# Next x late, routing early, block sums moved on VectorE, and the base bias added by GpSimd

## The reference, cut to what matters

```python
w = weight[adapter_ids]                        # one of 8 matrices, 1024 x 1024, for each batch element
y = einsum('bsi,boi->bso', x, w)               # x: 8 elements x 256 tokens x 1024
base_out = y @ base_W.T + base_b
logits = y @ router_W.T + router_b             # 15 experts, mapped onto 8
probs = softmax(logits)                        # the 8 largest kept, summed by mapped expert: gates
h = y @ A.T                                    # 8 experts x rank 16 = 128 columns
lora = ((h * gate) @ B) * 2.0
out = x + base_out + lora
```

## Time and profile before

| | us |
|---|---|
| median of 3 runs | 430.16 (429.05 to 432.26) |
| profiled execution: time | 432.55 |
| profiled execution: span from first to last instruction | 430.7 |
| busy in the span: PE, PEld, DVE, ACT, POOL | 404.3, 373.5, 295.6, 154.9, 0.8 |
| mean granted TensorE clock | 0.988 of full speed |

### The profile page before, as it was taken

One profiled execution on the slowest core, in us unless ns is written; L12 is line 12 of the kernel. 1 busy time (PEld: TensorE's weight loads), 2 busy tenths in 40 slices (PEclk: granted clock), 3 DMA queues, 4 the chain that ended last, 5 costly groups with the idle time before them and its releaser, 6 DMA issues.

```text
span 430.7 us, 6373 instructions
## 1 busy us (share of the span) xinstructions
PE 404.3 (94%) x2272; PEld 373.5 (87%) x2272; DVE 295.6 (69%) x577; ACT 154.9 (36%) x238; POOL 0.8 (0%) x8
## 2 busy tenths in 40 slices
PE   6989969998599998999999999999999999999997
PEld 5869869877598898989899898988989898988996
DVE  2586996788736886389844998369863898449643
ACT  3466325571104631166202642056401652035200
POOL 0000000000000000000000000000000000000000
PEclk9999999999599999999999999999999999999999
DMA  6999403771015740276204760157402762055002
GB/s 200 384 299 390 151 1 148 266 226 45 0 50 202 284 147 0 97 278 219 88 0 174 282 226 0 49 218 269 146 0 110 289 211 72 0 195 195 2 2 97
DMA packets 25598, 64.73 MB, mean 150 GB/s; under 512 B 2546, under 2 KB 11634, under 8 KB 25586
## 3 DMA queue, kind: packets, MB, share of 16 engines
q1 hardware_dynamic: 25586, 64.57, 42.4%
HBM read 56.18 MB, written 8.39 MB: 150 GB/s over the span
## 4 chain that ended last, share of the span: by engine, by line
PE 61%; DVE 21%; ACT 6%; issue 6%; DMA 5%; SPq 1%; DVEq 0%; ACTq 0%
PE y_ps L726 22%; PE y_ps L728 11%; DMA w_raw<-in_wT 5%; PE x_ps L761 4%; PE x_ps L763 4%; PE x_ps L762 4%; DVE w_lo L458 3%; ACT w_hi L357 3%; DVE res L555 3%; DVE x_split L464 3%; ACT x_split L367 1%; PE y_ps L738 1%; PE z_ps L762 1%; PE z_ps L761 1%; PE z_ps L763 1%
## 5 line engine op out<-in xcount | busy, mean ns | idle before, releaser
L726 PE MATMUL y_ps<-x_split,w_hi 128*128 128x512 f32 x496 | 173.1, 395 | 3.1 <-DVE y_sum L470 2.9
L728 PE MATMUL y_ps<-x_split,w_lo 128*128 128x256 f32 x496 | 137.6, 277 | 0.0
L726 PEld LDWEIGHTS y_ps<-x_split,w_hi 128*128 128x128 f32 x496 | 93.0, 188 | 25.6 <-issue 3.1
L728 PEld LDWEIGHTS y_ps<-x_split,w_lo 128*128 128x128 f32 x496 | 93.2, 188 | 0.0
L458 DVE TENSOR_TENSOR w_lo<-w_raw,w_hi 128x1024 fp32r<-128x1024 f32 x62 | 75.7, 1224 | 16.5 <-ACT w_hi L357 14.4
L357 ACT CAST w_hi<-w_raw 128x1024 fp32r<-128x1024 f32 x62 | 64.8, 1049 | 14.4 <-DMA w_raw<-in_wT 14.3
L349 ACT COPY y_sum<-y_ps 128x256 f32<-128x256 f32 x62 | 23.1, 372 | 115.7 <-PE y_ps L728 115.7
L470 DVE TENSOR_TENSOR y_sum<-y_ps,y_sum 128x256 f32<-128x256 f32 x62 | 26.1, 421 | 30.3 <-ACT y_sum L349 29.7
L749 PE MATMUL pl_ps<-pl_hi,y_hi 128*128 128x432 f32 x128 | 46.0, 359 | 0.0
L750 PE MATMUL pl_ps<-pl_lo,y_hi 128*128 128x432 f32 x128 | 45.8, 358 | 0.0
L751 PE MATMUL pl_ps<-pl_hi,y_lo 128*128 128x432 f32 x128 | 45.8, 358 | 0.0
(11 more groups left out here) (136 smaller groups left out, 608.0 us busy)
## 6 DMA issues: line engine op xcount, KB each, us to landing
w_raw<-in_wT SPq DMA_DIRECT2D x63, 512.0 KB, 3.3
res<-in_x SPq DMA_DIRECT2D x16, 512.0 KB, 4.2
out<-res SPq DMA_DIRECT2D x15, 512.0 KB, 2.6
x_raw<-in_xT SPq DMA_DIRECT2D x14, 512.0 KB, 6.1
hi_raw<-in_base_t SPq DMA_DIRECT2D x4, 368.0 KB, 6.1
st_raw<-in_base_t SPq DMA_DIRECT2D x4, 368.0 KB, 6.8
pl_raw<-in_base_t SPq DMA_DIRECT2D x2, 576.0 KB, 6.4
x_raw<-in_xT SPq DMA_DIRECT2D x4, 256.0 KB, 4.1
```

Source lines behind the costliest of these rows:

```text
L726: nc.tensor.matmul(y_ps[:, c % 2, :], w_hi[:, s, k, :], x_split[:, k, :, :].rearrange("p s t -> p (s t)"), start=(k == 0), stop=False)
L728: mm = nc.tensor.matmul(y_ps[:, c % 2, 0:T], w_lo[:, s, k, :], x_split[:, k, 0, :], start=False, stop=(k == KC - 1))
```

## The change

The base bias leaves VectorE: `add_bias` now stands in GpSimd's program, two adds for each element. VectorE's order in an element becomes: the fourth sum and its split, the routing up to the exponential, the first add from x_ps, the gates, two adds, the split of hw, and only then `make_x_lo`. In element 1 the split of the fourth sum is also put behind the split of hw. ScalarE takes the exponential before the next x. In element 0 the routing comes before the block differences, and the split of hw and b before the next x and the next weights; the splits of A, router and plain columns stand two chunks later. SyncE issues the two loads of `res` after the weight loads of chunks 4 and 5, not 2 and 3. TensorE's three waits for the T splits are each put before the product that needs them.

```diff
@@ sync, element
-                    if c in (2, 3):
-                        load_res(b, c - 2)
+                    if c in (4, 5):
+                        load_res(b, c - 4)
@@ scalar, element
                 fourth_hi(b)
+                exponential(b)
                 if not last:
                     make_x_hi(b + 1)
-                exponential(b)
                 make_hwt_hi(b)
@@ scalar, element 0 (the same on vector with ar_lo, plain_lo)
-                if c == 2:
+                if c == 4:
                     ar_hi()
-                if c in (3, 4):
-                    plain_hi(c - 3)
+                if c in (5, 6):
+                    plain_hi(c - 5)
             for h in range(2):
                 blocks_hi(h)
+            exponential(0)
             make_x_hi(1)
-            exponential(0)
             act.wait_ge(b_in, 16)
             act.wait_ge(ar_lo_done, 2)
             nc.scalar.copy(b_hi[:, :], b_raw[:, :]).then_inc(b_hi_done, 1)
+            make_hwt_hi(0)
             for c in range(OC, OC + 3):
                 adapter_hi(0, c)
-            make_hwt_hi(0)
@@ vector, stage2
-                routing_logits(b)
                 dve.wait_ge(res_biased, 2 * b + 2)
...
                 make_hwt_lo(b)
+                if isinstance(b, int) and b == 1:
+                    fourth_lo(b)
+                if not last:
+                    make_x_lo(b + 1)
@@ vector, element
                     t34_lo()
-                add_bias(b)
-                fourth(b)
-                if not last:
-                    make_x_lo(b + 1)
-                fourth_lo(b)
-                stage2(b)
+                    fourth(b)
+                    routing_logits(b)
+                else:
+                    fourth(b)
+                    fourth_lo(b)
+                    routing_logits(b)
+                stage2(b, last)
@@ vector, element 0
             masks()
-            block_sums_1_2()
-            add_bias(0)
             routing_logits(0)
             routing_gates(0)
-            make_x_lo(1)
+            block_sums_1_2()
+            make_hwt_lo(0)
             dve.wait_ge(b_hi_done, 1)
             nc.vector.tensor_tensor(b_lo[:, :], b_raw[:, :], b_hi[:, :], ALU.subtract).then_inc(b_lo_done, 1)
+            block_sums_3_4()
+            make_x_lo(1)
             for c in range(OC, OC + 3):
                 adapter_lo(0, c)
-            make_hwt_lo(0)
-            block_sums_3_4()
@@ tensor, stage2
-                pe.wait_ge(t_lo_done, 3)
+                pe.wait_ge(t_lo_done, 1)
...
                 product(z_ps, s_block(S1), T1).then_inc(z_ps_done, 1)
+                pe.wait_ge(t_lo_done, 2)
...
                 product(w_ps, y_block(1, 0), B10)
+                pe.wait_ge(t_lo_done, 3)
@@ gpsimd
+            def add_bias(b):
+                for t in range(NT):
+                    pool.wait_ge(res_in[t], 16 * (b + 1))
+                    nc.gpsimd.tensor_tensor(res[:, t, :], res[:, t, :], bias[:, :], ALU.add).then_inc(res_biased, 1)
+
+            pool.wait_ge(small_in, 48)
+            add_bias(0)
+            with pool.Fori(1, NB) as b:
+                add_bias(b)
```

More of the change, by code:

```diff
@@ L550, in make_hwt_lo @@
                                         ALU.subtract).then_inc(hwt_lo_done, 1)
[L552 to L555, removed]
             def add(t, cols, ps):
@@ L563, in add_plain, with stage2 @@
                     add(t, PLAIN, pl_ps[:, t, AR:PL]).then_inc(pl_added, 1)
-            def stage2(b):
-                routing_logits(b)
+            def stage2(b, last):
                 dve.wait_ge(res_biased, 2 * b + 2)
@@ L683, in _ @@
                     adapter_lo(0, c + 3)
-                if c == 2:
+                if c == 4:
                     ar_lo()
-                if c in (3, 4):
-                    plain_lo(c - 3)
+                if c in (5, 6):
+                    plain_lo(c - 5)
             blocks_lo(0)
```

## The result

| | median of the runs, us | lowest to highest | profiled execution | its span |
|---|---|---|---|---|
| before | 430.39 | 429.05 to 432.26 | 432.55 | 430.7 |
| after | 438.96 | 435.19 to 443.32 | 435.19 | 433.4 |

The ratio after to before is 1.0167 (95% interval 1.0088 to 1.0246): the change makes the kernel 0.9 to 2.5% slower, where 416.5 (408 to 437) was forecast. The profiled execution after is its shortest; two others, with a mean granted clock of 0.977 and 0.980 instead of 0.988, have spans of 437.1 and 437.2.

What follows compares the result with a forecast made beforehand. TensorE was taken as the bound, busy 404.3 of 430.7 us, so only its idle time and clock could change. Terms -5.4, -9.2, -6.1 and +7.0 for GpSimd's hold sum to -13.7, forecast 416.5 us, range 408 to 437.

Steps and rivals of the forecast that it cites:

- the hold of VectorE by GpSimd's adds: Stage 1, VectorE beside GpSimd's two adds: held 2.4 us an element, steady elements stall 1.0, element 1 loses 2.0; +7.0 in all.
- upper bound of 4.6: Longest hold of VectorE an element: whole length of two GpSimd adds, 1.6 to 2.3 us each, scaled from 128x128 rows.
- the sum was near +1: Whole kernel, if the two skill pages hold: hold near the upper bound, total change about +1 us.
- The second rival: VectorE shut out for each add's whole length, 2 x 2.3 us; GpSimd costs 22.5, sum +1.8, 432 (426 to 437); chance 0.31.
- The room of 1.46 us: VectorE's fullest stretch before the plain products: 0.5 idle plus 0.96 until y_lo is wanted; more hold stops TensorE one for one.
- the third rival: Hold as in the second rival, plus TensorE's clock falling to 1.2 GHz in elements 2 to 6, 2.8 each: 446; chance 0.13.
- Steady elements without GpSimd: Elements 2 to 6: TensorE's wait at x_ps for VectorE's add goes, -1.22 us each, -6.1 in all.
- Element 0: Stalls for hw and its split go, -4.7; fewer y_sum waits in stage 1, -0.7; sum -5.4 us.
- Element 1: Wait at x_ps falls from 7.0 to about 0.2, -6.8; clock drop goes, -2.8; weight load +0.4; sum -9.2 us.
- The weight load behind the store: Element 1's first weight load stands behind SyncE's store of element 0's token half 1: 0.4 us more stall than before.
- All without GpSimd's cost: Whole kernel were it not for GpSimd's adds: -5.4 - 9.2 - 6.1 = -20.7 us.

Runs made afterwards that it cites:

- write-only kernel: The changed kernel with each GpSimd add replaced by a fill of the same res rows with zeros; one run, 410.81 us, span 409.0.
- first experiment: The changed kernel with its bias adds back on VectorE, all other moves kept; 414.55 us, ratio 0.962 to the kernel before, span 413.0.

## Why the prediction was wrong

**The step that failed is the hold of VectorE by GpSimd's adds**, the term "2.4 us an element, +7.0". I priced it by VectorE's own add of 2.36 for two, as the nearest row of the same operation. It was 4.07 to 4.2 in a steady element, near the upper bound of 4.6 that came from GpSimd's own small rows times eight. VectorE's row says nothing of GpSimd's speed, and the hold is paid at GpSimd's. The Trainium skill's page "SBUF — State Buffer" (Who interferes with whom) states the mutual exclusion; this case's trace agrees, with 2.21 and 1.86 us added to two splits. From the time that the Trainium skill's page "GPSIMD Engine Reference" (3.1 Elementwise) gives for an add of twice the size came an estimate of 2.2 us an add; the 2.21 agrees. By the two pages the sum was near +1. My own upper bound of 4.6 gave much the same, so the likeliest case should have been the second rival, which I gave 0.31 against my 0.36.

**The room of 1.46 us was right**, for three sizes of the hold: 4.07, 4.24 and 3.41 less 1.46 are 2.61, 2.78 and 1.95, and TensorE waits 2.61, 2.77 and 1.95. With the true hold a steady element loses 3.0 and gains 1.3, in place of 1.0 and 1.2.

**The clock**, part of the third rival, came true in three of six elements, at 1.6 us where two neighbours can be compared. I had given the stalls of 3.1 us at least 2.8 each in five elements, hence 446: the number and the size were both too high. The second rival's cost of GpSimd, 22.5, stands against 24.4, the span after less that of the write-only kernel. By their gates 6.3 of it lie up to element 1 (forecast 2.0 + 4.0), 18.1 in elements 2 to 6, two drops of the clock among it (15.5, which counted no drop), nothing in element 7 (1.0). So the profiled execution came out 2.6 us above the one before, where that rival had +1.8. The median is 8.6 above; by the estimate above, more drops of the clock account for 3 to 5 us of it, but no trace of those runs tells in which elements. Why a stall of 2.6 us brings the clock down in elements 2 and 3 and not in 4 to 6 stays open.

**Steady elements without GpSimd**: -1.22 predicted, -1.32 measured (50.0 to 48.68). Right, and the later x alone gives it.

**Element 0**: right. Its low-rank product was forecast at 56.2:

```profile
56.28 0.44 PE L773 MATMUL z_ps<-b_hi,hwt_hi 128*128 128x368 f32 x1 [0.32 <-DVE b_lo L695]
```

The 1.59 us wait for hw is gone as well, and the next element's first product begins at 63.22 (forecast 63.1). GpSimd costs 0.7 there, where I had put nothing: with writing alone it begins at 62.51.

**Element 1**: the 6.8 us wait and the clock drop behind it go, as said. In the kernel after nothing is left at x_ps (0.2 forecast); with the bias back on VectorE 1.4 us remain. The weight load behind the store was under-priced: +0.4 forecast, while the waits between chunks there rise from about 1.0 us to 3.6 in the kernel after (0.78 and 2.82) and 2.4 with the bias on VectorE. I had seen the store in front of the load, but not that 2.1 us pass between them, as in the kernel before (69.60 to 71.70).

**All without GpSimd's cost**: -20.7 forecast. The write-only kernel's span is 21.7 below that before, and the first experiment's, which pays for the bias on VectorE, 17.7. That part of the working stands. GpSimd's adds cost 24.4 us against writing alone, where I had priced them at 7.0, and 20.4 against having them on VectorE.

## What to carry to other kernels

Work moved from VectorE to GpSimd is not off VectorE: while GpSimd reads two SBUF tensors, VectorE's instructions with two SBUF inputs stand still, so price the move at GpSimd's duration, not VectorE's, and only what is left after the room counts. Here 2.35 us of VectorE became 4.07. If such an add must be on GpSimd, put its load so late that it falls behind the last value that TensorE waits for: holds of the same length then cost 17 us less here, the drops of the clock included.

## What was unexpected of the hardware

- Not only instructions with two SBUF inputs are held. In element 0 beside GpSimd's adds, a cast of 15 elements with one input took 2.37 us, where it took 0.17 with the write-only GpSimd, 0.30 beside the one-input multiplication and 1.27 beside the halved adds:

```profile
41.37 3.89 DVE L607 TENSOR_TENSOR st_lo<-st_raw,st_hi 128x1472 fp32r<-128x1472 f32 x1
...
45.18 2.37 DVE L612 CAST map_f<-map_i 128x15 f32<-128x15 int32 x1
```

- The add with one input in PSUM (y_sum, 0.41 us) was not held beside the same adds.
- GpSimd's multiplication with one input is shown for 6.2 us for two, yet lengthens VectorE's instructions by 0.84 and 0.39 only, and one of writing alone (0.95 us) by nothing. The length that the profile shows for GpSimd is not the length of the hold.
- Cut into halves, the adds hold VectorE for less: 3.4 us for four against 4.07 for two, since more of their turns fall beside instructions that are not held.
- Stalls of TensorE of one length do not always bring the clock down: after 2.4 to 2.8 us in three of six elements of one execution, after 1.95 us in one of six.
